# The attended product copied at the head of ScalarE's next step, its low half taken behind VectorE's output sum

## What is computed

```python
x = x + L0_xattn(layernorm(x), ctx, Wq, bq, Wk, bk)
x = x + L0_ffn(layernorm(x), W, b, A, B, gate_w, gate_b)          # dense, plus a routed low-rank part
x = x + L1_xattn(layernorm(x), ctx, mask, q_proj, k_proj, v_proj, o_proj, q_norm, k_norm)
x = x + L1_ffn(layernorm(x), gate/up/down as 4-bit weights with zeros and scales)

# L1_xattn: 32 query heads of 128, 8 key/value heads, each shared by 4 query heads
q = rmsnorm(x @ Wq.T); k = rmsnorm(ctx @ Wk.T); v = ctx @ Wv.T    # per head
out = softmax(q @ k.T * scale + mask) @ v
return out @ Wo.T
```

## Time and profile before

| | |
|---|---|
| median of three runs | 985.12 us |
| profiled execution | 986.86 us, its span 985.1 us |
| TensorE matmul busy | 876.9 us, 89% |
| VectorE, ScalarE, GpSimd busy | 555.0, 492.5, 510.9 us |
| stage of the 64 steps, first to last `attend()` | 242.0 to 779.1 us |

### The profile page before, as it was taken

The page is one execution under the profiler, slowest core; times in us unless marked ns, Lnnn a source line. Parts: engine busy times, 40 slices in busy tenths (PEclk is TensorE's granted clock), DMA queues, the critical chain, the costliest instruction groups (busy, mean ns, idle before and its releaser), DMA issues.

```text
span 985.1 us, 14600 instructions
## 1 busy us (share of the span) xinstructions
PE 876.9 (89%) x4096; PEld 716.9 (73%) x4096; DVE 555.0 (56%) x1072; ACT 492.5 (50%) x1776; POOL 510.9 (52%) x559
## 2 busy tenths in 40 slices
PE   7999999999788888888888888888864699999996
PEld 5786887877677777777777777777743578888885
DVE  6316424324455555555555555555563469889987
ACT  4543831336566566666665556666542234444442
POOL 4323431225666666666666666666443235666662
PEclk9999999999899999999999999999977789999999
DMA  7401110125555555555555555555722014333312
GB/s 252 159 22 55 33 55 6 38 65 152 159 161 161 161 161 161 160 163 162 163 163 164 163 163 163 161 163 166 268 85 85 34 76 150 141 134 133 132 57 86
DMA packets 75238, 126.37 MB, mean 128 GB/s; under 512 B 8429, under 2 KB 46061, under 8 KB 75182
## 3 DMA queue, kind: packets, MB, share of 16 engines
q1 hardware_dynamic: 75182, 125.74, 41.3%
HBM read 90.06 MB, written 35.65 MB: 128 GB/s over the span
## 4 chain that ended last, share of the span: by engine, by line
PE 77%; issue 8%; DVE 5%; POOL 4%; DMA 3%; ACT 2%; SPq 1%; DVEq 0%; ACTq 0%; POOLq 0%
PE bank L1203 20%; PE bank L1205 19%; PE bank L1204 19%; PE bank L1434 5%; PE bank L1371 3%; PE bank L1372 3%; PE bank L1400 2%; PE bank L1401 2%; PE bank L1220 1%; DMA land<-block_bounce 1%; DVE st L882 1%; DMA resid<-in_x_dram 1%; POOL prob L551 1%; DVE xnT_lo L907 1%; PE bank L1321 1%
## 5 line engine op out<-in xcount | busy, mean ns | idle before, releaser
L575 POOL TENSOR_TENSOR probT_lo<-land,probT_hi 128x512 fp32r<-128x512 f32 x64 | 82.2, 1285 | 184.4 <-ACT probT_hi L766 184.4
L760 ACT ACTIVATE aoT_hi<-bank 128x512 fp32r<-128x512 f32 x64 | 38.2, 598 | 191.5 <-PE bank L1205 191.5
L1057 DVE TENSOR_TENSOR aoT_lo<-bank,aoT_hi 128x512 fp32r<-128x512 f32 x64 | 44.2, 691 | 128.3 <-ACT aoT_hi L760 128.3
L1203 PE MATMUL bank<-split,xnT_hi 128*128 128x512 f32 x288 | 114.8, 399 | 1.9 <-DVE xnT_lo L907 1.9
L1205 PE MATMUL bank<-split,xnT_lo 128*128 128x512 f32 x288 | 112.8, 392 | 0.0
L1204 PE MATMUL bank<-split,xnT_hi 128*128 128x512 f32 x288 | 112.6, 391 | 0.0
L1203 PE MATMUL bank<-split,aoT_hi 128*128 128x512 f32 x256 | 105.0, 410 | 6.6 <-DVE resid L1014 6.6
L1204 PE MATMUL bank<-split,aoT_hi 128*128 128x512 f32 x256 | 103.9, 406 | 0.0
L1205 PE MATMUL bank<-split,aoT_lo 128*128 128x512 f32 x256 | 103.4, 404 | 0.0
L1203 PE MATMUL bank<-probT_hi,vcur_hi 128*128 128x512 f32 x64 | 31.3, 490 | 74.0 <-issue 48.0
L773 ACT ACTIVATE prob<-bank,nmax 128x128 f32<-128x128 f32 x256 | 90.2, 370 | 2.4 <-DVE nmax L1050 2.4
(11 more groups left out here) (151 smaller groups left out, 2272.3 us busy)
## 6 DMA issues: line engine op xcount, KB each, us to landing
block_bounce<-tb SPq DMA_DIRECT2D x244, 128.0 KB, 2.3
land<-block_bounce SPq DMA_DIRECT2D x61, 512.0 KB, 3.5
raw<-in_wqo_dram SPq DMA_DIRECT2D x62, 256.0 KB, 3.0
kv<-in_ffn_w_dram SPq DMA_DIRECT2D x14, 768.0 KB, 4.4
kv<-in_ffn_z_dram SPq DMA_DIRECT2D x14, 768.0 KB, 5.5
kv<-in_up_s_dram SPq DMA_DIRECT2D x14, 256.0 KB, 5.7
resid<-in_x_dram SPq DMA_DIRECT2D x2, 1024.0 KB, 9.2
kv<-in_ctx_dram SPq DMA_DIRECT2D x1, 2048.0 KB, 10.4
```

The costliest lines, as they stand in the source:

```text
L575: pool.tensor_tensor(by_head(probT_lo[:]), landed(i + PLAG, 1), as32(by_head(probT_hi[:])), ALU.subtract).then_inc(s_ptl, 1)
L1203: pe.matmul(dst, l_hi, r_hi, start=first, stop=False)
```

## The change

On ScalarE the copy `aoT_hi` leaves its place behind `headT`; the copy of step j is now the first instruction of step j, where it was in the middle of step j-1. On VectorE `aoT_lo` of step j now follows the reciprocal and `add_out(j-1)` of step j, where it was the last of step j-1. The waits of both and their signals stay the same for the same data. TensorE, GpSimd and SP are not touched, and no instruction is added or removed.

```diff
@@ ScalarE, step(j, p)
                 def valid(k):
                     return 0 <= k and (p is not None or k < STEPS)
+                if valid(j):
+                    act.wait_ge(s_e, at(p, j) + 1)
+                    if p is not None or j >= 1:
+                        act.wait_ge(s_f, at(p, j))
+                    act.activation(aoT_hi[:], bank[6][:], ACT.Copy).then_inc(s_ah, 1)
                 if valid(j + LEAD - 1):
@@
-                if valid(j + 1):
-                    act.wait_ge(s_e, at(p, j + 1) + 1)
-                    if p is not None or j >= 0:
-                        act.wait_ge(s_f, at(p, j + 1))
-                    act.activation(aoT_hi[:], bank[6][:], ACT.Copy).then_inc(s_ah, 1)
                 if valid(j + 2):
@@ VectorE, step(j, p)
                 if valid(j - 1):
                     add_out(j - 1, p)
+                if valid(j):
+                    dve.wait_ge(s_ah, at(p, j) + 1)
+                    dve.tensor_tensor(aoT_lo[:], bank[6][:], as32(aoT_hi[:]), ALU.subtract).then_inc(s_al, 1)
                 if valid(j + 3):
@@
-                if valid(j + 1):
-                    dve.wait_ge(s_ah, at(p, j + 1) + 1)
-                    dve.tensor_tensor(aoT_lo[:], bank[6][:], as32(aoT_hi[:]), ALU.subtract).then_inc(s_al, 1)
```

## The result

The changed kernel took 900.69 us, the median of four runs (898.3 to 902.24), beside 985.32 us for the kernel before on the same chip: a ratio of 0.914, with a 95% interval of 0.910 to 0.918. Forecast were 903 us and a range of 893 to 925. The profiled execution has a span of 897.5 us, 87.6 less than before; the sum had said 83.9.

A forecast was written before the change was run, and what follows sets the result against it. TensorE's wait before attend(), about 1.04 us an inner step, was taken to bound the kernel; 54.0 + 4.4 + 2.5 + 17.1 + 5.9 = 83.9 us off the profiled 986.86 gave 903 us, range 893 to 925.

The forecast's parts named there:

- The bound and its chain: Inner steps: TensorE loses 1.04 us before attend(), ended by a 4.36 us chain from output product's end through aoT_hi to vcur_lo.
- The inner steps: Fifty periods fall from 8.11 to 7.03 us each, TensorE's own work plus transitions: gain 54.0 us.
- the ring above: From the experiments, ScalarE's move alone: loop from mask through exponentials, aoT_hi, aoT_lo, multiply, transposes to next mask, 7.33 us.
- The start: Five periods before 287.03, same chain beside chunk loads and a lower TensorE clock: gain 4.4 us, bounds 2 and 6.
- The weight loads: Steps while the units' weights load, where a slower bounce must be waited out: gain 2.5 us, bounds 0 and 4.
- The last steps: From attend 58 to output product 61, chain wholly exposed without the query product: gain 17.1 us, bounds 8 and 20.
- The end: From output product 61 on, statistics and norms no longer behind aoT_lo of 63: gain 3.9 + 2 = 5.9 us, bounds 3 and 7.
- The range: Whole kernel: 893 to 925 us, holding the forecast's own range of 893 to 917 and (a).
- (a): Rival: the last steps don't shorten, held by norms, GpSimd products and TensorE's low clock; 4 instead of 23.0, 922 us; chance 0.15.
- (b): Rival: the bounce becomes the bound; inner period 7.55 us, inner steps give 28 instead of 54, 929 us; chance 0.13.
- (d): Rival: slower through the bounce, from 10.3 us write to landing; at 11.4 in every step 997 us; chance 0.03.
- The rule weighed: VectorE instructions with two SBUF inputs wait out GpSimd instructions reading SBUF; weight subtractions kept at 3.44 us, aoT_lo not affected.

The follow-up runs named there:

- second profile: The changed kernel itself, profiled once more with the last group of experiments; median there 901.08 us, 50 inner periods in 352.04 us.
- spread loads: Changed kernel with the first two units' weights loaded in single transfers over steps 40 to 57, not all in 53 and 54: 898.19 us, later 898.72.

## Why the prediction was right, point by point

**The bound and its chain.** Right, and shown from two sides: 34 us of the inner steps' 54 go when only ScalarE's copy is moved, and 45 when only GpSimd's order is changed.

**The inner steps.** 54.0 forecast, 53.6 measured; the cover of 1.5 us for `vcur_lo` is 1.59 (413.23 to 414.82), and no stall of TensorE is left. But the part on VectorE was weighed wrongly. I costed `aoT_lo` behind the sum at up to 0.1 us and saw only cost in that move; without it the period is 7.34 by the ring above. The sum came out since both moves were in the change, not since each was understood (the layout of both together fits row by row, as shown above): 20 us of this term hang on a move that I had booked as a mere cost.

**The start.** 6.0 for 4.4, at the upper bound. The second profile has attend 5 at 282.49, a gain of 4.5, and with other kernels of the same order there it lies between 280.3 and 283.0: the excess is no larger than the scatter of the start.

**The weight loads.** 1.3 for 2.5 (1.5 in the second profile). The mechanism was right, as the spread loads show. The size was off: I let the two steps lose 1.4 and 0.9 us; they lose 1.5 and 1.8 against 7.03 (8.55 and 8.79), 1.0 us more; and the waits of the kernel before were 4.6 us there (25.65 less 21.09), not the 4.8 that I summed.

**The last steps.** 19.4 for 17.1: attends 59, 60, 61 and output product 61 came 7.6, 6.5, 7.0 and 7.6 us apart, for 8.1, 7.4, 7.0 and 8.5. Of the half microsecond at attend 59, 0.2 is the weight work, 3.21 us for 3.44. Another part is TensorE's clock: I let the output product of 58 run at the low clock, and in this execution it stayed at 2.4 GHz behind a wait of 3.03 us. The clock is not the whole: in the second profile it did fall in that product, and the stretch took 29.7 us, for 28.7 and my 31.0. So about 1.0 of the 2.3 us was the clock's luck, and the rest are links that I had made too long.

**The end.** 3.8 and 3.5 for 3.9 and 2.0, together 7.3 where my upper bound was 7. The granted clock behind output product 63 is 0.99 for 0.97; in the second profile it is 0.98 and this last stretch gains 2.5.

**The range.** All lower bounds together give 925, not the 917 that the prediction calls the end of the forecast's own range; the stated range reached to 925 anyway, and the measurement lies far from it.

**The rivals.** (a) would have left 4 us in the last steps; 26.7 are there. (b), the bounce as the bound, didn't come true, and the run with 2.07 us more shows how near it is: of 2.07 us, 1.31 came through in two steps (2 x 0.65), so 0.8 were slack, where I had 1.1. For (d), slower, the bounce would have to take 10.3 us from write to `headT` in every step; only the two steps of the weight loads had that (11.1 us from 626.12, 12.8 from 633.15).

**The rule weighed.** The two subtractions took 3.21 us in the changed kernel, beside GpSimd, and `aoT_lo` 0.69 beside the multiply. By the rule of the Trainium skill ("SBUF — State Buffer", "Who interferes with whom") the trace agrees in both. It holds for the other side as well: `vcur_lo` on GpSimd took 0.90 us beside such a subtraction, for 0.46 otherwise (next section).

## What to carry to other kernels

When an engine runs a fixed order, look for an instruction that waits for the far end of the pipeline and ask what stands behind it that could have run; move it to the point where its wait is over anyway. Then close the ring: follow the new order through both queues until it comes back to its start, since a ring of two queues can set the period with no engine full, and a move that looks like a mere cost on the second engine may be what opens it. And write down which transfer's slack paid for the gain: 2 us more on this bounce cost nothing in the old inner steps and 33 us in the new ones.

## What the runs showed of the hardware

At the turn of the hardware loop (16 steps), twice in a run, ScalarE stands still with no releaser in the profile: 1.8 to 2.1 us in the changed kernel and with ScalarE's move alone, where `aoT_hi` heads the step, 0.6 and 1.3 us in the kernel before, where the squares do. With ScalarE's move alone:

```profile
394.38 0.60 ACT L734 ACTIVATE aoT_hi<-bank 128x512 fp32r<-128x512 f32 x1 [1.90 <-issue]
```

In the ring that became 2.1 and 2.2 us of the period; in the changed kernel, with slack, 0.3.

Waits of about 3 us left TensorE's clock sometimes high, sometimes low. In the changed kernel the output product that followed a wait of 3.32 us (from 679.26) ran at 0.23 us a matmul, 2.4 GHz; after 3.94 us it began so and fell to 0.43, 1.2 GHz, a microsecond into the work:

```profile
679.26 0.39 PE L1203 MATMUL bank<-split,aoT_hi 128*128 128x512 f32 x1
679.49 0.40 PE L1204 MATMUL bank<-split,aoT_hi 128*128 128x512 f32 x1
...
686.10 0.50 PE L1203 MATMUL bank<-split,aoT_hi 128*128 128x512 f32 x1 [3.94 <-DVE aoT_lo L1028]
...
687.19 0.63 PE L1204 MATMUL bank<-split,aoT_hi 128*128 128x512 f32 x1
687.62 0.63 PE L1205 MATMUL bank<-split,aoT_lo 128*128 128x512 f32 x1
```

With the spread loads, the same attend 59 after the same 3.03 us was at 1.2 GHz at once (0.76 us for its first matmul). And in the second profile of the changed kernel the product that ran at 0.23 us above came, after the same wait of 3.32 us, at 0.43 (granted clock 0.50):

```profile
681.57 0.63 PE L1203 MATMUL bank<-split,aoT_hi 128*128 128x512 f32 x1
682.00 0.63 PE L1204 MATMUL bank<-split,aoT_hi 128*128 128x512 f32 x1
```

So the same kernel and the same wait gave both levels.

A GpSimd instruction can be the one that is held (0.90 us for 0.46), when VectorE's subtraction of two SBUF inputs came first (658.15 to 659.90, above):

```profile
659.32 0.90 POOL L555 TENSOR_TENSOR vcur_lo<-kv,vcur_hi 128x128 fp32r<-128x128 f32 x1
...
666.01 0.46 POOL L555 TENSOR_TENSOR vcur_lo<-kv,vcur_hi 128x128 fp32r<-128x128 f32 x1 [0.86 <-ACT vcur_hi L785]
```
